# One block for projection and attention, regrouped maximum units and split memsets in a transformer layer on one core

## What is computed

```python
x = x + 0.5 * ffn(layernorm(x))          # blockwise FP4, hidden 704
x = x + attention(layernorm(x))          # 16 heads of 16, causal
x = x + 0.5 * ffn(layernorm(x))
# attention: q, k, v = z @ Wq.T, z @ Wk.T, z @ Wv.T
# softmax(mask(q k^T / 4)) v, then @ Wo.T
```

## Time and profile before

| | us |
|---|---|
| median of 3 runs | 2062.61 |
| lowest and highest | 2060.91, 2064.49 |
| the profiled execution | 2063.07 |
| its span | 2061.3 |
| first feed-forward | up to about 490 |
| projection, last PE product ends | 677.39 |
| attention, first PE product starts | 680.14 |

### The profile page before, as it was taken

How to read it: one execution, slowest core, us unless ns; L and a number is a source line. 1 busy time by engine, 2 the same in 40 slices (tenths; PEclk the granted TensorE clock), 3 DMA queues, 4 the chain that set the end, 5 groups by cost and what they waited for, 6 DMA issues and landing times. The chain is left out here.

```text
span 2061.3 us, 44210 instructions
## 1 busy us (share of the span) xinstructions
PE 1980.3 (96%) x13211; PEld 1300.5 (63%) x13211; DVE 1838.4 (89%) x4649; ACT 1342.6 (65%) x2323; POOL 1088.4 (53%) x1773
## 2 busy tenths in 40 slices
PE   4999999998998999999999999999998899999999
PEld 3888888887776433333333333333327788888888
DVE  7899999998687799999999999999946899999997
ACT  4455454545776788888888888888894345555553
POOL 6788888885644222222222222222221788888885
PEclk9999999999999999999999999999999999999999
DMA  6000000001855645555555455555426000000000
GB/s 208 20 0 0 0 0 0 0 0 57 250 192 192 147 133 140 140 138 147 143 142 134 138 137 139 139 138 147 111 77 215 6 16 20 20 20 20 15 21 26
DMA packets 134841, 185.02 MB, mean 90 GB/s; under 512 B 24928, under 2 KB 76512, under 8 KB 134368
## 3 DMA queue, kind: packets, MB, share of 16 engines
q1 hardware_dynamic: 132000, 182.11, 31.0%
q10 hardware_dynamic: 2688, 1.05, 0.2%
HBM read 113.90 MB, written 85.98 MB: 97 GB/s over the span
## 5 line engine op out<-in xcount | busy, mean ns | idle before, releaser
L1915 POOL TENSOR_SCALAR_AFFINE_SELECT diag_scores<-diag_scores 128x256 f32<-128x256 f32 (+1 forms) x320 | 148.3, 463 | 676.7 <-ACT diag_scores L1885 668.3
L1388 DVE CUSTOM_DVE_ANT_0 gu_ps<-gu_ps,mask_qk 128x256 f32<-128x256 f32 (+3 forms) x690 | 339.9, 527 | 47.5 <-PE gu_ps L1373 39.9
L1373 PE MATMUL gu_ps<-k_stack,q_stack 96*128 96x512 bf16 (+3 forms) x1050 | 318.4, 335 | 9.3 <-DVE part_max L1388 5.4
L1822 PE MATMUL gu_ps<-probs,v_group 128*17 128x512 f32 (+3 forms) x3072 | 310.1, 491 | 3.0 <-ACT probs L1891 1.8
L935 PE MATMUL gu_ps<-wguT_hi,ffn_xT_hi 128*128 128x512 f32 (+1 forms) x768 | 309.8, 403 | 1.1 <-DVE ffn_xT_lo L704 1.1
L935 PE MATMUL gu_ps<-wguT_hi,ffn_xT_lo 128*128 128x512 f32 (+1 forms) x768 | 287.8, 375 | 0.0
L935 PE MATMUL gu_ps<-wguT_lo,ffn_xT_hi 128*128 128x512 f32 (+1 forms) x768 | 287.4, 374 | 0.0
L919 ACT ACTIVATE ffn_z<-xs,ffn_shift,ffn_rstd 128x256 f32 (+1 forms) x128 | 76.9, 601 | 322.7 <-POOL ffn_shift L786 322.7
L1887 ACT ACTIVATE probs<-hT_ps 128x256 f32<-128x256 f32 (+2 forms) x320 | 259.7, 811 | 12.4 <-PE hT_ps L1798 11.7
L1373 PEld LDWEIGHTS gu_ps<-k_stack,q_stack 96*128 96x128 bf16 x1050 | 95.6, 97 | 268.0 <-DVE part_max L1388 188.7
L1887 ACT ACTIVATE probs<-av_ps 128x256 f32<-128x256 f32 (+2 forms) x320 | 263.6, 824 | 0.7 <-PE av_ps L1803 0.6
(11 more groups left out here) (221 smaller groups left out, 4903.1 us busy)
## 6 DMA issues: line engine op xcount, KB each, us to landing
q_stack<-q_parts SPq DMA_DIRECT2D x192, 128.0 KB, 3.4
k_stack<-k_parts SPq DMA_DIRECT2D x192, 128.0 KB, 3.5
o_all<-o_sb SPq DMA_DIRECT2D x64, 256.0 KB
q_parts<-qkv_parts SPq DMA_DIRECT2D x32, 384.0 KB, 2.8
k_parts<-qkv_parts SPq DMA_DIRECT2D x32, 384.0 KB, 3.9
v_ones<-qkv_vst SPq DMA_DIRECT2D x16, 544.0 KB, 3.9
v_group<-v_ones SPq DMA_DIRECT2D x32, 272.0 KB, 4.2
xs<-in_L_attn_x SPq DMA_DIRECT2D x8, 1024.0 KB, 7.8
```

The lines of the kernel that those rows point to most:

```text
L1373: mm = T.matmul(out[:, e, :], qs[0:STACK, h0 + e, t * P:(t + 1) * P], ks[0:STACK, h0 + e, c * CHUNK:c * CHUNK + w], start=True, stop=True)
L1388: last = V.tensor_tensor_reduce(out=ps[:, e * w:(e + 1) * w], in0=ps[:, e * w:(e + 1) * w], in1=mask_qk[:, CHUNK - w:CHUNK], scale=1.0, sc ...
L1822: mm = T.matmul(o_ps[h * VPAD:h * VPAD + VCOLS, CHUNK - w:CHUNK], vs[:, t, h, :], probs[:, h // 2, i % 2, h % 2, at:at + w], start=first, ...
L1915: G.affine_select(out=block_of, in_=block_of, compare_op=ALU.is_ge, fill=MASKED, base=0, pattern=[[0, 2], [0, count], [1, P]], channel_mul ...
```

## The change

1. The maximum units are regrouped. The v products are cut in four tiles with a slot ahead of each; units stand one each ahead of v tiles 1, 2 and 3 and two ahead of q/k part 0 of the next chunk. On DVE, the reductions of those two come ahead of the statistics. The transposes now wait for the units ahead of part 0. `turn_max` moves from chunk 13 to the second unit place ahead of part 0 of chunk 14, with `m_hi` at the start of chunk 14 on ACT and `m_lo` on DVE behind the reductions.
2. Each memset of two rows by four heads becomes four of one head each. Those of groups 0 and 1 stand at the ends of chunks 2 to 9, those of groups 2 and 3 behind the first four causal selects of attention groups 0 and 1.
3. Projection and attention become one block. The barrier of all engines between them goes; in its place PE waits for the last rest (`hT_ps` is free then), for ACT's last copy of v ahead of pair B, for `cleared` ahead of its first product with v, and DVE for its own last reduction ahead of its memset.

```diff
 # qkv_vector
             def rests(js):
                 for j in js:
-                    head_reduced(dve, c, f"qk{j}")
+                    if j:
+                        head_reduced(dve, c, f"qk{j}")
...
+            head_reduced(dve, c, "qk0")
             if has_chunk(c + 2):
                 qkv_statistics(dve, c + 2)
+            if c == TURN_CHUNK:
+                m_lo(dve, 0, 0, head_bank(TURN))
             rests((0,))
...
-            for u in range(2):
-                head_reduced(dve, c, f"v{u}")
+            for t in range(CT):
+                head_reduced(dve, c, f"v{t}")
 # qkv_gpsimd
             if c in STACK_ENDS_AT:
-                r = STACK_ENDS_AT.index(c)
                 qkv_part_done(pool, "lo", c, 3, 4)
-                G.memset(ring[r][1][STACK:STACK_MAX, :, :], -1.0).then_inc(att_sem["filled"], 1)
-                pool.wait_ge(att_sem["filled"], r + 1)
+                fill_ends(pool, *divmod(STACK_ENDS_AT.index(c), GROUP))
+        def fill_ends(pool, r, h):
+            G.memset(ring[r][1][STACK:STACK_MAX, h, :], -1.0).then_inc(att_sem["filled"], 1)
+            pool.wait_ge(att_sem["filled"], r * GROUP + h + 1)
 # qkv_tensor
             for u in range(2):
-                head_units(pe, c, f"v{u}")
                 qkv_part_done(pe, "v_sb", c - 1, u, 2)
                 for t in range(2):
+                    head_units(pe, c, f"v{2 * u + t}")
 # qkv_scalar
+            if c == TURN_CHUNK:
+                m_hi(act, 0, 0, head_bank(TURN))
             highs((0, 1))
...
-                if (c, f"v{u}") == (TURN_CHUNK, TURN_SLOT):
-                    m_hi(act, 0, 0, head_bank(TURN))
 # plan
-        for c in range(FIRST_AT, CHUNKS - 2):
-            HEAD_PLAN.update({(c, "v0"): 1, (c, "v1"): 2, (c + 1, "qk0"): 1, (c + 1, "qk1"): 1})
-        HEAD_PLAN.update({(CHUNKS - 2, "v0"): 2, (CHUNKS - 2, "v1"): 2, (CHUNKS - 1, "qk0"): 1, (CHUNKS - 1, "qk1"): 2,
-                          (CHUNKS - 1, "qk2"): 2, (CHUNKS - 1, "qk3"): 2, (CHUNKS - 1, "v0"): 1, (CHUNKS - 1, "v1"): 1})
+        for c in range(FIRST_AT, CHUNKS - 1):
+            HEAD_PLAN.update({(c, "v1"): 1, (c, "v2"): 1, (c, "v3"): 1, (c + 1, "qk0"): 2})
+        HEAD_PLAN.update({(CHUNKS - 1, "qk1"): 2, (CHUNKS - 1, "qk2"): 2, (CHUNKS - 1, "qk3"): 1, (CHUNKS - 1, "v1"): 1,
+                          (CHUNKS - 1, "v2"): 1, (CHUNKS - 1, "v3"): 1})
-        STACK_ENDS_AT = (3, 4)
+        STACK_ENDS_AT = range(2, 2 + 2 * GROUP)
 # head_banks_free: (c - 1, "qk1") becomes (c - 1, "qk0")
 # head_units: the wait for zT_lo of the next chunk moves from "v0" to "v1"
 # attention, PE
+                        projection["tensor"](pe)
+                        pe.wait_ge(qkv_sem["rest"], 4 * CHUNKS)
...
+                                if n == 0 and i == 0 and pair == 1:
+                                    pe.wait_ge(qkv_sem["v_sb"], 2 * CHUNKS)
...
-                        pe.wait_ge(s["cleared"], 2)
...
-                                pe.wait_ge(s["filled"], g + 1)
+                                pe.wait_ge(s["filled"], (g + 1) * GROUP)
...
+                                        if n == 0 and i == 1:
+                                            once(pe, "cleared", 0, 2)
                                         values(b, g, i - 1)
 # attention, SP, ACT, POOL: each stream begins with its part of the projection
 # attention, POOL
                                 causal(b, g, d)
...
-                            if b == 0 and g < 2:
-                                qkv_stored(pool)
-                                once(pool, "causal", 0, (n + 1) * (2 * len(DIAG)))
-                                G.memset(ring[g + 2][1][STACK:STACK_MAX, :, :], -1.0).then_inc(s["filled"], 1)
-                                once(pool, "filled", 0, g + 3)
+                                if n < 2 and d < GROUP:
+                                    qkv_stored(pool)
+                                    once(pool, "causal", n * (2 * len(DIAG)), 2 * d + 2)
+                                    fill_ends(pool, n + 2, d)
 # attention, DVE
+                        projection["vector"](dve)
+                        once(dve, "reduced", 0, NU + EARLY)
                         V.memset(o_ps[:, :], 1.0).then_inc(s["cleared"], 1)
```

More of the change, by code:

```diff
@@ L1280, in qkv_scalar @@
             middles((0, 1))
-            if c == TURN_CHUNK + 1:
+            if c == TURN_CHUNK:
                 store_max(act, 0, 0)
@@ L1437, in build @@
         EARLY = 19
-        FIRST = ([("unit", 0, u) for u in range(NU)] + [("unit", 1, u) for u in range(4)] + [("turn_max", 0)]
-                 + [("unit", 1, u) for u in range(4, EARLY)])
+        FIRST = ([("unit", 0, u) for u in range(NU)] + [("unit", 1, u) for u in range(6)] + [("turn_max", 0)]
+                 + [("unit", 1, u) for u in range(6, EARLY)])
         TURN = FIRST.index(("turn_max", 0))
@@ L1452, in build @@
         TURN_CHUNK, TURN_SLOT = next(where for where, es in head_at.items() if TURN in es)
-        assert TURN_SLOT == "v1" and TURN_CHUNK < CHUNKS - 1
-        STACK_ENDS_AT = (3, 4)
+        assert TURN_SLOT == "qk0" and TURN_CHUNK < CHUNKS - 1 and TURN == head_at[TURN_CHUNK, "qk0"][-1]
+        STACK_ENDS_AT = range(2, 2 + 2 * GROUP)
         def head_bank(e):
@@ L1467, in head_banks_free @@
         def head_banks_free(pe, c):
-            for e in head_at.get((c - 1, "qk1"), ())[-1:]:
+            for e in head_at.get((c - 1, "qk0"), ())[-1:]:
                 head_bank_free(pe, e - 1)
@@ L1476, in head_units @@
                 kind, g, *which = FIRST[e]
-                if where == "v0" and has_chunk(c + 1):
+                if where == "v1" and has_chunk(c + 1):
                     qkv_done(pe, "zT_lo", c + 1)
@@ L1495, in head_reduced @@
                         finish_max(dve, 0, 0)
-                if e == TURN + 1:
-                    m_lo(dve, 0, 0, head_bank(TURN))
         def project_qkv():
@@ L1567, in attention, with vector, gpsimd, tensor @@
-        def attention():
+                def vector(dve):
+                    V.memset(vst_all[:, :, DH:VCOLS], 1.0).then_inc(s["ones"], 1)
+                    V.memset(part_max[:], MASKED).then_inc(att_sem["cleared"], 1)
+                    dve.wait_ge(att_sem["cleared"], 1)
+                    chunks(lambda *at: qkv_vector(dve, *at))
+                def gpsimd(pool):
+                    chunks(lambda *at: qkv_gpsimd(pool, *at))
+                def tensor(pe):
+                    chunks(lambda *at: qkv_tensor(pe, *at))
@@ new lines, in scalar, with sync, send_values, step @@
+                def scalar(act):
+                    act.wait_ge(s["ones"], 1)
+                    chunks(lambda *at: qkv_scalar(act, *at))
+                def sync(sp):
+                    def send_values(c, par):
+                        qkv_done(sp, "v_sb", c * 2 + 1)
+                        at = c % (SEQ_TILES // CT) * CT
+                        sp.dma_start(v_ones[c // (SEQ_TILES // CT), :, :, at:at + CT, :].rearrange("g p t c -> p g (t c)"),
+                                     vst[:, :, :, :, :].rearrange("p g t h d -> p g (t h d)")
+                                     ).then_inc(v_out[par], 16)
+                    def step(c, par, turn):
+                        for j in range(4):
+                            if j == 3:
+                                send_values(c, par)
+                            qkv_part_done(sp, "lo", c, j, 4)
+                            m = (j % 2) * P
+                            sp.dma_start(qk_parts[j // 2][:, m:m + P, bass.ds(c * CHUNK, CHUNK)]
+                                         .rearrange("a p c -> p a c"), parts[:, par, j, :, :]
+                                         ).then_inc(parts_out[par], 16)
+                        if c == 2:
+                            for of in range(2):
+                                sp.wait_ge(v_out[of], 16)
+                                sp.wait_ge(parts_out[of], 64)
+                            fill_stacks(sp, 0, 0, range(0, 3))
+                        if c == 3:
+                            fill_stacks(sp, 0, 0, range(3, 6))
+                            fill_values(sp, 0, 0)
+                        if 4 <= c < 7:
+                            fill_stacks(sp, 0, 1, range(2 * (c - 4), 2 * (c - 3)))
+                    chunks(step)
@@ L1570, in attention @@
+            return {"vector": vector, "gpsimd": gpsimd, "tensor": tensor, "scalar": scalar, "sync": sync}
+        def attention(projection):
             s = att_sem
@@ L1737, in _ @@
                     def _(sp):
+                        projection["sync"](sp)
                         qkv_stored(sp)
@@ L1826, in values @@
                             mm.then_inc(s["pv"], 1)
[L1828 removed]
                         def group(b, g, last):
+                            n = b * GROUPS + g
                             prev = before(b, g)
                             if b == 0:
[L1833 removed]
```

(7 more changed lines are left out.)

45 lines of the change are left out of this document (removed).

## The result

| | before, same chip | after |
|---|---|---|
| median of 4 runs | 2061.99 | 2044.55 |
| lowest and highest | 2060.91, 2064.49 | 2041.38, 2046.11 |
| the profiled execution, its span | 2063.07, 2061.3 | 2045.3, 2043.5 |

The ratio of after to before is 0.9912, with a 95% interval of 0.9895 to 0.9929: 17.4 us less by the medians, 17.8 by the two profiled executions. I had forecast 2049.6, 13.0 us less, and a range that began at 2045.0. The direction holds, the size was too small, and the range begins 0.45 us above the measured median.

The account below looks back on a forecast made before the run. Unit chunks were taken as bound by PE plus its waits, chiefly for DVE's reductions to free banks. First interval 5.8 + eight intervals 8.2 + tail 0.8 + boundary 0 - clock 1.8 = 13.0 us: 2049.6, range 2045 to 2055.

Parts of the forecast that it names:

- Eight intervals: Transposes to transposes, chunks 6 to 14: period 11.82 falls to 10.8 us, 8.2 us gained, bounds 4.5 and 10.
- One wait stays: PE's second unit ahead of q/k part 0 waits for the v tile 3 unit's bank: 0.45 us, bounds 0.2 and 0.9.
- First interval: First interval with units, from chunk 5's transposes: 17.03 falls to 11.2 us, 5.8 us gained, bounds 4.5 and 6.5.
- waits of 0.8: In the first interval with units, PE still waits 0.8 us because DVE is late there for one chunk.
- Tail: From chunk 14's transposes to the projection's last product, 20.42 us before: 0.8 us gained, bounds 0 and 1.5.
- The boundary: Projection to attention: 4.8 us gained up to step 5 becomes a wait of about 5 us for the fill, gain 0.
- rival (b): Fill isn't last to come at step 5, so the gain of up to 4.8 us counts: 2044.8, chance 0.08.
- the 1.8 forecast: Low clock behind PE's wait at step 5 of attention group 0: 1.8 us lost, bounds 0 and 2.5.
- (a): Bank waits move instead of going: intervals keep about 11.4 us, the eight give 3.4, time 2054.4; chance 0.10.
- (c): Reductions ahead of statistics delay `rstd`, DVE stands at the shift in every chunk: 18 us slower, 2067.6; chance 0.04.
- (d): Intervals stay because something other than the named waits bounds PE: within 0.2% of before, chance 0.02.

Follow-up runs that it names:

- e1: Before with the regrouped units alone, whole-group memsets and barrier kept: 2051.06 against 2063.92, ratio 0.9956.
- e2: Before with the split memsets alone: 2057.86 against 2063.92, ratio 0.9978.
- e3: Before with projection and attention as one block alone, units and memsets as before: 2064.29 against 2063.92, ratio 1.0008.
- e5: After, with the reductions of the pair ahead of q/k part 0 put back behind the statistics on DVE: 2042.75, before's median beside it 2063.06.
- e4: After with the barrier put back: 2042.68 against 2063.92, ratio 0.9907.
- e8: e7 with the reduction of the unit ahead of q/k part 0 behind the statistics on DVE: 2049.32, before's median beside it 2063.06.
- e7: After, with the two units ahead of q/k part 0 placed one ahead of part 0 and one ahead of part 1: 2054.74, before's median beside it 2063.06.
- e6: After, with SP filling group 2's stack behind the even chunks' stores alone, not all stores: 2040.17 against 2063.06, ratio 0.9894.
- e10: The kernel of e6 run once more: 2039.31 against 2064.05, ratio 0.9885.

## Why the prediction was right in kind and short in size

**Eight intervals: right mechanism, mis-sized term.** The step that failed is "One wait stays: the second unit of the pair needs the bank of the v tile 3 unit ... I take 0.45 with its restart". That wait is nearly nowhere: the weight loads of above waited 1.1 us in eight intervals, 0.14 each. PE and DVE of after at the end of chunk 11 and the start of 12:

```profile
614.40 0.39 PE L1380 MATMUL gu_ps<-k_stack,q_stack 96*128 96x512 bf16 x1
...
614.83 0.69 DVE L1400 TENSOR_REDUCE part_max<-gu_ps 128x1 f32<-128x512 f32 x1 [0.23 <-PE gu_ps L1380]
...
615.33 0.63 PE L1380 MATMUL gu_ps<-k_stack,q_stack 96*128 96x512 bf16 x2
...
615.87 0.70 DVE L1395 CUSTOM_DVE_ANT_0 gu_ps<-gu_ps,mask_qk 128x512 f32<-128x512 f32 x1 [0.35 <-PE gu_ps L1380]
...
617.14 0.14 DVE L1395 DVE_READ_ACCUMULATOR2_ANT part_max<- 128x1 f32 x1
```

The v tile 3 unit starts at 614.40; its reduction starts 0.43 later and takes 0.69, so the bank is free at 615.52, 1.12 us after the start. The second unit of the pair goes about 0.22 after the first, near 615.55: the bank is just free. I had added 0.39 of matmul, 0.68 of reduction and two hand-overs of 0.1 to 0.2 to about 1.4. The matmul and the reduction were right, and the mis-sized term is the hand-overs: 0.04 us from the matmul's end, as listed, to the reduction, and about 0.03 back, as in the row that I had named for it (`rstd`'s end at 552.30, the shift at 552.33). The price that I took from the double unit in before, 0.20, was not a turn-around at all. DVE of before, at that place:

```profile
590.00 1.40 DVE L1161 TENSOR_TENSOR qkv_rest<-hT_ps,qkv_parts 128x512 f32<-128x512 f32 x2
591.32 1.88 DVE L1393 TENSOR_REDUCE part_max<-gu_ps 128x1 f32<-128x512 f32 x3
```

The unit of 589.83 was long done when DVE came to its reduction at 591.32, behind the two rests of parts 2 and 3, with no idle time between; here DVE idles 0.23 us for PE ahead of the reduction. So my lower bound of 0.2 for that wait should have been none, and with it my upper bound of 10 us for the eight intervals, which measured 10.83, was too low. Without the 0.45 my own sum, 9.26 + 1.1 = 10.36, is 0.11 from the measured 10.47, and over eight intervals these 0.9 us are about that 1.1.

**First interval.** 6.70 us gained, 5.8 forecast, 6.5 the upper bound. The step that failed is "waits of 0.8, because DVE is still late there for one chunk". DVE isn't late: it comes to the shift at 548.91 after `rstd` is done, and from 546 to 555.8 it is DVE that waits, 0.60 us for ACT ahead of the low part of the transposes and 0.5 for PE ahead of two reductions, while PE waits for nothing. e1 and e2 show the two causes, 5.34 from the memset and 1.36 from the regrouping.

**Tail.** 1.33 gained, 0.8 forecast, inside its bounds. No run takes this stretch apart.

**The boundary.** The mechanism was right: PE starts at once, the fill starts 5.1 us after PE's end of projection, the gain becomes a wait at step 5 (4.12 us, 4 to 6 forecast), and the clock falls behind it. PE reaches step 5 4.6 us earlier after its end of projection than before (14.31 against 18.89), 4.8 forecast. So rival (b) is excluded, though the time came out near its 2044.8, which is a coincidence, and e3 shows the mechanism alone. The loss was smaller than the 1.8 forecast: B is 0.75 longer than before. It has two parts. From step 5 to `turn_max` took 31.29 us against 29.68, so 1.61 lost behind the wait, close to 1.8. And the fill took 13.34 us in place of 14.20, 0.86 given back, which I had not allowed for; since its length varies by 2 us from execution to execution, that part is luck. The last two columns of the ledger show the first part over all kernels: with waits up to 1.23 us the rest of B takes 29.7 to 30.3 us, with waits of 3.2 to 5.5 us 31.0 to 32.5. It goes with the low clock: where that took 3.4 us behind step 5 (after, e3, e5) the rest is 31.0 to 31.3, where it took 5 to 6.5 us (e4, e8, e7) 32.0 to 32.5. The Trainium skill (TensorE: Matmul & The Clock Gate, HAM oscillation — how this bites in real kernels) says that a wait for DMA leaves the next matmuls at half rate; the trace agrees, with the 4.12 us of wait and PEclk 0.66 in the 5 us behind it. It needs no DMA, though: the two rows that I named in the prediction were waits for DVE and at the barrier, and in e5, e6 and e10 the clock fell behind a wait of 1.47 us for ACT.

**The sum.** 6.70 + 10.83 + 1.33 - 0.75 = 18.11 against 13.0; the span fell by 17.8. Of the 5.1 us missed, 2.6 are the eight intervals, 0.9 the first, 0.5 the tail and 1.05 the boundary. All four went the same way. The first two have one reason: I charged PE with waits for DVE, 0.45 and 0.8 us for an interval, and with the new plan DVE frees each bank just in time. Rivals (a), (c) and (d) are excluded: no interval is above 10.7, no idle time of DVE at the shift, and the intervals did not stay. The share of DVE that rival (a) gives is wrong: 71.42 of 94.60 us are 75%, not 79, and it rose to 87% (72.75 of 83.70) without a wait of the transposes. e4 keeps the barrier and runs as fast as after, so the boundary term of zero stands too.

What stays open is the worth of the barrier with an early fill, 1.5 us by single profiled executions and 0.8 by medians, and what decides where the clock falls. With the late fill B differs by 1.1 us to the barrier's favour (e3 against before) and by 2.6 against it (e4 against after), but PE waits at step 5 in all four, so these are the fill's length and the clock.

## What to carry to other kernels

A wait at a shared PSUM bank is priced by what stands ahead of the reduction on DVE, not by the reduction alone: before you charge a turn-around from a row of the old kernel, look whether the releasing engine was busy with something else or idle, and take the hand-overs from rows too. Put the work that PE must not wait for far ahead of where its result is needed; here 7.4 of the 10.83 us of eight intervals came from moving one unit of each chunk ahead by six products. A barrier whose idle time lies ahead of a load that starts by another chain is worth nothing until that chain is moved: find what starts the load first. And when a wait shrinks, look whether its releaser came earlier or the waiting engine came later: in e6 it was both.

## What the runs showed of the hardware

- The fill of one stack, 12 loads and the v load, took 13.34 to 15.47 us from its first issue to the release of PE, with the same instructions. From 7.6 to 7.8 us of that is SP issuing the twelve loads ahead of the v load (8.6 in e6 and e10), and 5.7 to 7.6 us pass from the v load's issue to the release. The lengths: 13.34 (after), 13.70 (e3), 14.02 (e5), 14.20 (before), 14.55 (e8), 14.75 (e7), 15.19 (e4), 15.12 and 15.47 (e10 and e6, where the last store is still on its way as the fill begins).
- A store to DRAM released SP 3.98 to 4.00 us after its issue in all kernels that wait for it, with or without a barrier between.
- The low clock doesn't follow the length of the last wait alone. Behind the barrier's idle stretch of 2.32 us PEclk is 0.51 over 10 us in e1 and 1.00 over 10 us in e4. Behind a wait of 1.47 us for ACT it is 0.59 over the next 4.2 us in e5 and e10, and likewise low in e6, and 1.00 in after, e7 and e8; after and e6 have the same waits of 0.29 and 0.2 us ahead of it and no longer ones. What else decides was not tried.
- A bank was free again 1.12 us after the start of a unit of 512 columns, with the reduction of 0.69 us in it: 0.39 of matmul as listed, 0.04 to the reduction's start.
